# Rotating the next group's queries right behind their product, ahead of the squares and of gating, in a fused gated-attention and feed-forward kernel

## The reference, cut to what matters

```python
# 16 sequences of 64 tokens, 256 wide; 16 query heads in 4 groups, head width 128
xn = layernorm(x)
q = rms_norm(xn @ wq, q_norm_w); k = rms_norm(xn @ wk, k_norm_w); v = xn @ wv
k_ctx = rms_norm(ctx @ wk_ctx, k_norm_w); v_ctx = ctx @ wv_ctx
q = q * cos + rotate_half(q) * sin          # the rotation; k likewise, k_ctx not
scores = q @ concat(k_ctx, k).T / sqrt(128) + causal_mask
x = x + tanh(g_xattn) * (softmax(scores) @ concat(v_ctx, v)).flat @ wo
h = layernorm(x)                            # the weights below rounded to 8-bit floats
x = x + tanh(g_ffn) * ((silu(h @ gate * gs) * (h @ up * us)) @ down * ds)
```

## Time and profile before

| | |
|---|---|
| three runs | 312.31, 312.32, 313.82 us; median 312.32 |
| the profiled execution | 312.29 us, of which the span from first to last instruction is 310.2 us |
| TensorE clock granted | 1.00 of full speed in the whole span |
| busy: PE, DVE, ACT, POOL | 294.8 (95%), 229.4 (74%), 232.2 (75%), 180.8 us (58%) |
| HBM | 40 GB/s over the span; transfers are dense only in its first eighth |

### The profile page before, as it was taken

The page is one execution under the profiler, slowest core; times in us unless marked ns, Lnnn a source line. Parts: engine busy times, 40 slices in busy tenths (PEclk is TensorE's granted clock), DMA queues, the critical chain, the costliest instruction groups (busy, mean ns, idle before and its releaser), DMA issues.

```text
span 310.2 us, 6558 instructions
## 1 busy us (share of the span) xinstructions
PE 294.8 (95%) x2231; PEld 234.8 (76%) x2231; DVE 229.4 (74%) x481; ACT 232.2 (75%) x893; POOL 180.8 (58%) x177
## 2 busy tenths in 40 slices
PE   6896989998999999999999999999999999988876
PEld 3354656675877888888888888888888888877765
DVE  1668998889888898769875787758775976676553
ACT  2468687887789978888977768787887778776632
POOL 1225695567747687457955586457755685556330
PEclk9999999999999999999999999999999999999999
DMA  6999000000000010000000010000000000000001
GB/s 200 389 389 394 15 17 2 0 1 2 18 3 0 1 36 2 0 0 21 19 0 2 0 37 0 2 1 20 0 3 0 2 17 4 2 0 19 0 0 36
DMA packets 6720, 12.84 MB, mean 41 GB/s; under 512 B 800, under 2 KB 4256, under 8 KB 6688
## 3 DMA queue, kind: packets, MB, share of 16 engines
q1 hardware_dynamic: 6688, 12.43, 11.3%
HBM read 11.38 MB, written 1.05 MB: 40 GB/s over the span
## 4 chain that ended last, share of the span: by engine, by line
PE 31%; ACT 27%; DVE 25%; issue 8%; POOL 6%; DMA 2%; SPq 1%; DVEq 0%; POOLq 0%
ACT probs L932 10%; ACT squares L768 6%; PE ps_y L444 5%; DVE row_max L1217 4%; DVE exp_bias L1220 3%; DVE q_sin L1082 3%; PE ps_attn L737 3%; PE ps_transposed L430 3%; ACT qt L852 3%; PE ps_scores L693 3%; DVE q_rot L1078 2%; PE ps_kv L418 2%; ACT const L825 2%; PE ps_probs L430 2%; DMA const<-in_constants_dram 2%
## 5 line engine op out<-in xcount | busy, mean ns | idle before, releaser
L932 ACT ACTIVATE probs<-ps_scores,exp_bias,q_scale 128x128 f32<-128x128 f32 x128 | 57.0, 456 | 26.5 <-DVE exp_bias L1220 26.4
L1395 POOL TENSOR_TENSOR q_rot<-q_rot,q_sin 128x512 f32<-128x512 f32 x31 | 39.7, 1281 | 17.6 <-DVE q_sin L1082 17.5
L1439 POOL TENSOR_TENSOR probs<-probs,row_inv 128x512 f32<-128x512 f32 x32 | 36.3, 1134 | 19.0 <-DVE row_inv L1273 19.0
L1346 POOL TENSOR_TENSOR q_scale<-ssq_eps,minus_half 128x4 f32<-128x4 f32 x32 | 38.8, 1213 | 10.5 <-DVE ssq_eps L1243 9.8
L1357 POOL TENSOR_TENSOR fuse_lo<-fuse,fuse_hi 128x256 fp32r<-128x256 f32 x21 | 15.4, 733 | 41.8 <-ACT fuse_hi L777 41.8
L768 ACT ACTIVATE squares<-ps_q 128x128 bf16<-128x128 f32 x128 | 34.1, 292 | 5.9 <-PE ps_q L412 4.1
L737 PE MATMUL ps_attn<-pt,values 128*128 128x256 f32 x128 | 33.4, 383 | 0.0
L693 PE MATMUL ps_scores<-kt,qt 128*64 128x128 f32 x512 | 33.3, 273 | 0.0
L1078 DVE TENSOR_TENSOR q_rot<-ps_q,rope 128x512 f32<-128x512 f32 x31 | 21.2, 684 | 11.9 <-ACT squares L768 11.9
L693 PEld LDWEIGHTS ps_scores<-kt,qt 128*64 128x64 f32 x512 | 28.9, 137 | 0.0
L908 ACT ACTIVATE pt<-ps_probs 128x512 f32<-128x512 f32 x32 | 19.2, 600 | 11.8 <-PE ps_probs L430 11.6
(11 more groups left out here) (190 smaller groups left out, 832.0 us busy)
## 6 DMA issues: line engine op xcount, KB each, us to landing
q_raw<-in_wq_dram SPq DMA_DIRECT2D x4, 512.0 KB, 8.7
o_raw<-in_wo_dram SPq DMA_DIRECT2D x4, 512.0 KB, 11.6
ctx_t<-in_ctx_dram SPq DMA_DIRECT2D x8, 128.0 KB, 2.6
out_dram<-x_sb SPq DMA_DIRECT2D x8, 128.0 KB, 1.9
stage<-in_gate_w_dram SPq DMA_DIRECT2D x2, 384.0 KB, 10.4
stage<-in_up_w_dram SPq DMA_DIRECT2D x2, 384.0 KB, 11.4
x_sb<-in_x_dram SPq DMA_DIRECT2D x1, 768.0 KB, 13.4
stage<-in_down_w_dram SPq DMA_DIRECT2D x2, 384.0 KB, 13.1
```

The lines of the kernel that those rows point to most:

```text
L932: last = nc.scalar.activation(probs[:, i, :], ps_s[:, i * P:(i + 1) * P], ACT.Exp, bias=exp_bias[:, i:i + 1], scale=q_scale[:, k % 2, i:i ...
L1346: return nc.gpsimd.tensor_tensor(dst, src, minus_half[:, 0:src.shape[1]], ALU.pow)
L1395: nc.gpsimd.tensor_tensor(q_rot[:, :, :], q_rot[:, :, :], q_sin[:, :, :], ALU.add)\
L1439: nc.gpsimd.tensor_tensor(probs[:, :, :], probs[:, :, :], row_inv[:, :].unsqueeze(2).broadcast_to([P, 4, P]), ALU.mult).then_inc(probs_rea ...
```

## The change

It moves three things and turns one dependence round. VectorE rotates the queries of k + 1 as soon as their product is made (`q_made`), ahead of the next tile's norm, `k_var`, gating and the keys' rotation; only `ot_lo` and, at j = 2, L1147 stay in front. ScalarE's squares of the same queries wait for the rotation (`q_sin_ready`) where the rotation waited for them; TensorE's next product into `ps_q` waits for the squares, and `ssq_eps` too. GpSimd adds the queries ahead of `fuse_rest` and the keys' sum. ScalarE makes `x2t_hi` ahead of the keys' squares. No instruction is added or removed.

```diff
--- before.py
+++ after.py
@@ -642,10 +642,7 @@
                     g1 = (k + 1) % GROUPS
                     p1 = ((k + 1) // GROUPS) % 2
                     if is_step(u, k):
-
-                        pe.wait_ge(q_sin_ready, step(u, k) + 1)
-                    if at_step(u, k) == 0:
-                        pe.wait_ge(q_squared, 1)
+                        pe.wait_ge(q_squared, step(u, k) + 1)
                     q_tile = tile(u, (k + 1) // GROUPS)
                     is_native = native("q", g1, q_tile)
                     weights_ready("q", g1, q_tile)
@@ -800,7 +797,7 @@
                 m, j = divmod(k, GROUPS)
                 par, nxt = m % 2, (m + 1) % 2
                 if is_step(u, k + 1):
-                    act.wait_ge(q_made, step(u, k + 1) + 1)
+                    act.wait_ge(q_sin_ready, step(u, k + 1) + 1)
                     if is_step(u, k):
                         act.wait_ge(ssq_moved, step(u, k) + 1)
 
@@ -875,6 +872,11 @@
                 if not after_last:
                     fuse_high(u, FF_LATE.get(k - 1))
 
+                if j == 2 and is_tile(u, m - 1):
+                    act.wait_ge(x2_turned, tile(u, m - 1) + 1)
+                    nc.scalar.activation(x2t[0][:, (m - 1) % 2, :, :].rearrange("p c n -> p (c n)"), ps_t[:, 0:HID], ACT.Copy)\
+                        .then_inc(x2_hi_ready, 1)
+
                 if j == 2 and is_tile(u, m + 1):
                     t1 = tile(u, m + 1)
 
@@ -893,10 +895,6 @@
                     if tile(u, m + 1) >= TOKENS_SPLIT_FROM:
                         nc.scalar.activation(xt[0][:, nxt, 0:KC, :].rearrange("p c n -> p (c n)"), ps_t[:, 0:HID], ACT.Copy)\
                             .then_inc(xt_hi_ready, 1)
-                if j == 2 and is_tile(u, m - 1):
-                    act.wait_ge(x2_turned, tile(u, m - 1) + 1)
-                    nc.scalar.activation(x2t[0][:, (m - 1) % 2, :, :].rearrange("p c n -> p (c n)"), ps_t[:, 0:HID], ACT.Copy)\
-                        .then_inc(x2_hi_ready, 1)
                 if j == 3 and is_tile(u, m + 1):
                     act.wait_ge(ks_turned, tile(u, m + 1) + 1)
                     nc.scalar.activation(kt[:, nxt, :, 0:4:3, :],
@@ -1072,7 +1070,7 @@
                 par, nxt = m % 2, (m + 1) % 2
                 if is_step(u, k + 1):
 
-                    dve.wait_ge(q_squared, step(u, k + 1) + 1)
+                    dve.wait_ge(q_made, step(u, k + 1) + 1)
                     if is_step(u, k):
                         dve.wait_ge(q_turned, step(u, k) + 1)
                     nc.vector.tensor_tensor(q_rot[:, :, :], four(ps_q), over_heads(rope[:, 0, :]), ALU.mult)\
@@ -1148,6 +1146,8 @@
                                             ALU.subtract, ALU.mult).then_inc(x2_ready, 1)
 
 
+                rotate_queries(u, k)
+
                 if j == 3 and is_tile(u, m + 2):
                     dve.wait_ge(ln_inv_ready, tile(u, m + 2) + 1)
 
@@ -1186,8 +1186,6 @@
                         dve.wait_ge(ks_turned, tile(u, m) + 1)
                     nc.vector.tensor_tensor(kn[:, :, :], four(kv_bank(u, m + 1, 0)),
                                             k_inv[:, :].unsqueeze(2).broadcast_to([P, HPG, DIM]), ALU.mult).then_inc(kc_ready, 1)
-
-                rotate_queries(u, k)
 
                 if j == 2 and is_tile(u, m - 1):
                     dve.wait_ge(x2_hi_ready, tile(u, m - 1) + 1)
@@ -1240,6 +1238,7 @@
                 if is_step(u, k + 1):
                     if is_step(u, k):
                         dve.wait_ge(q_scale_ready, step(u, k) + 1)
+                    dve.wait_ge(q_squared, step(u, k + 1) + 1)
                     nc.vector.tensor_scalar(ssq_eps[:, :], ssq[:, :], DIM * RMS_EPS, None, ALU.add)\
                         .then_inc(ssq_moved, 1)
 
@@ -1380,6 +1379,12 @@
                     inverse_root(k_inv[:, :], k_var[:, :]).then_inc(kc_inv_ready, 1)
 
 
+                if is_step(u, k + 1):
+                    pool.wait_ge(q_sin_ready, step(u, k + 1) + 1)
+                    nc.gpsimd.tensor_tensor(q_rot[:, :, :], q_rot[:, :, :], q_sin[:, :, :], ALU.add)\
+                        .then_inc(q_rot_ready, 1)
+
+
                 fuse_rest(u, FF_LATE.get(k - 1))
 
 
@@ -1388,12 +1393,6 @@
                     pool.wait_ge(ks_roped, t1 + 1)
                     nc.gpsimd.tensor_tensor(k_cos[:, :, :], k_cos[:, :, :], k_sin[:, :, :], ALU.add)\
                         .then_inc(ks_added, 1)
-
-
-                if is_step(u, k + 1):
-                    pool.wait_ge(q_sin_ready, step(u, k + 1) + 1)
-                    nc.gpsimd.tensor_tensor(q_rot[:, :, :], q_rot[:, :, :], q_sin[:, :, :], ALU.add)\
-                        .then_inc(q_rot_ready, 1)
 
 
                 if ROUND_AT.get(k - 1, 0) >= WIDE:
```

## The result

The changed kernel takes 320.55 us (median of 4 runs, 319.69 to 320.57) against 312.31 us before: ratio 1.0246, 95% interval 1.0225 to 1.0267. The forecast was 318.7 us in a range of 315.5 to 321.5; the measured loss is 8.2 us where 6.4 were summed. The profiled execution took 320.57 us, of which the span is 318.4 us; before it was 312.29 and 310.2.

What follows compares the result with a forecast made beforehand. The prediction took TensorE, busy without a gap in steps 10 to 27, as the bound; 5.3 + 0.9 + 0.6 - 0.4 = +6.4 us on 312.3 gave 318.7 us, range 315.5 to 321.5.

Steps and rivals of the forecast that it cites:

- TensorE sets the pace of the middle: Steps 10 to 27: TensorE is busy throughout, so nothing ahead of it gains time; only a new wait loses some.
- The rival that the loop sets the pace: Steps 10 to 27: the chain's loop, not TensorE, sets step time; 10.4 us less, about 302 us; chance 5%.
- Steps with j = 2: Steps 10, 14, 18, 22, 26: TensorE waits for late keys' squares; +5.3 us, bounds 4.0 and 6.5.
- The prediction's estimate by the Trainium skill: Five j = 2 steps: if each VectorE operation waits for an empty pipe, 1.5 us more; not adopted.
- Steps with j = 1: Steps 17, 21, 25: `k_var` behind the rotation delays the context keys 0.3 us each; +0.9, bounds 0 and 1.5.
- Gating, `exp_bias`, GpSimd: nothing in the middle: Middle steps: gating's delay stays within 1.46 us of cover; earlier `exp_bias` and later GpSimd work change nothing.
- The first steps: 17 to 104 us: `q_rot` wait goes, step 1 gives it back, later squares delay TensorE; +0.6, bounds -2.0 and +3.
- the prediction's own sign: First 104 us: the forecast counts as wrong if this stretch changes by more than 2 us.
- The last steps: After the middle: waits for `qt` and L1147 shrink, most lost again in the last rotation step; -0.4, bounds -1.5 and +0.5.

Runs made afterwards that it cites:

- e8: Changed kernel with the new order and dependence only in steps with j = 2, the old one in all others: 318.50 us.
- e1: Changed kernel with the old order and dependence in steps with j = 2 alone: 313.41 us, ratio to before 1.0024.
- e7: Kernel before, with VectorE at j = 2 multiplying the keys by cosines and sines once more into spare buffers, ahead of the keys' rotation: 319.82 us.
- e2: Changed kernel with the old order and dependence in steps with j = 1 alone: 316.63 us.
- e6: Changed kernel with GpSimd's sum and `x2t_hi` back at their old places in every step: 321.48 us.
- e3: Changed kernel with the old order and dependence in step 1 alone: 318.17 us.
- e4: Changed kernel with six added TensorE multiplications of ones in step 1, ahead of its wait for the context keys: 318.82 us.
- e5: Changed kernel with the new order and dependence only in steps with j = 0 and j = 3, the old one otherwise: 309.72 us, ratio to before 0.9918.

## Why the prediction was right, point by point

**TensorE sets the pace of the middle.** Shown. Steps 15, 19, 23 and 27 take 8.56 us in all kernels shown, whatever ScalarE, VectorE and GpSimd do, and ScalarE's shorter wait for `exp_bias` bought nothing there. The exponentials did start 0.8 to 1.1 us sooner behind their scores in the steps from 15 to 27 with j = 3, 0 and 1 (0.3 later with j = 2). The rival that the loop sets the pace had to make such steps shorter by 0.8 us; steps 16, 20 and 24 got 0.05 shorter, as they did in e8, where their order is the old one.

The Trainium skill's caution against the matmul busy share ("Perfetto Trace Analysis", section "Identifying the Most-Contended Engine") did not bear here: a weight-load share of 87% came with no room for orders on the other engines.

**Steps with j = 2: +5.3.** Step 18's chain was forecast nearly start for start: rotation 0.09 us behind the product's end (0.04 measured, since L1145 was early), TensorE 4.81 us behind the query product measured and 4.81 forecast. That the two agree to the last digit is luck: the rotation came 0.05 us early and the handover to TensorE, 0.1 by choice, took 0.14. The five steps lengthened by 0.77 and 4 x 1.13, 5.3 in all. Shown by e1 (undone alone), e8 (done alone) and e7 (the pair alone).

The prediction's estimate by the Trainium skill, 1.5 us more over the five steps, did not come: the scaling starts 1.20 us behind the rotation, as in the rows before. The same section, "The DRAIN you can't avoid" in "VectorE: DVE Perf Modes", adds that a next operation that is not held starts earlier, which the prediction left out; so the rows don't speak against the page.

**Steps with j = 1: +0.9.** 0.08 in step 13 and 3 x 0.32, 1.05 in all; shown by e2.

**Gating, `exp_bias`, GpSimd: nothing in the middle.** Right, by the rows of step 20, the waits, and e6.

**The first steps: +0.6.** This is the term that was mis-sized: from step 0 to 10 it measured +2.2. By the prediction's own sign, a change of more than 2 us in the first 104, this part of the forecast was wrong, although the total was not. The waits came nearly as taken, which is in part luck, since +0.6 was an estimate with no row for each step behind it: -0.7 for `q_rot`, +0.8 in step 1, -0.9 for GpSimd's late division in step 3, +0.9 for the context keys in step 5 and +0.4 in steps 2 and 6, together about +0.5. What the sum lacked is the clock. I gave back in step 1 what was won in step 0, and looked at when the keys come, not at how long TensorE stands idle before them: 1.33 us before, 2.52 after, and behind that the granted clock fell to half for 3.4 us, at 1.7 us (e3, e4). The +2.2 stayed in the bounds that I gave, -2 to +3, which had no term for the clock.

**The last steps: -0.4.** -0.6. What `exp_bias` gives is mostly lost again, by two waits. The one that was forecast is in step 31: TensorE's wait for `qt` grew from 0.74 to 1.24 us behind the step with the rotation at j = 2 (it is 0.74 in e5, which has the old order there). The other, 0.69 us for `fuse_lo` in step 29, was not forecast, so the size is right in part by luck.

**The remainder** is the 0.5 us by which step 0 began later in the profiled execution, which no term had. The long first product that makes it is in four of the ten profiles, whatever the order.

## What to carry to other kernels

Where one engine is busy without a gap, moving work forward on another can hardly gain and can lose; ask which signal of the full engine has the least slack (here 0.16 us, the keys' squares) and what the moved work now stands in front of. An order that is harmful in two of four kinds of steps can be worth keeping in the other two: measured apart, j = 0 and 3 gave 0.8% and j = 1 and 2 took it and more. Count a new idle stretch of TensorE at the start twice, once for itself and once for what the clock may do behind it; the second is a chance and not a certainty.

## What the runs showed of the hardware that was not expected

Behind 2.52 us without work TensorE was granted 1.2 GHz for 3.4 us, in all four runs of the changed kernel (granted clock 0.995; only the profiled run shows where) but only in five of eight of e1 and three of four of e6, which have the same idle stretch. The four 128x512 products then took 3.19 us instead of 1.88. Behind 1.33 us (e2, e3, e5, e8) and behind 1.55 us with six small matrix products ahead of them (e4) it kept 2.4 GHz in all 21 runs. The idle stretch is not the only way to such a drop, though. One of four runs of e7 and, of the 19 runs of the kernel before made beside the experiments at a clock above 0.99, two had a granted clock of 0.994 or 0.995, with 1.33 us idle in their profiles; the two took 313.62 and 313.81 us. Where the clock fell in them no profile shows.

VectorE's `exp_bias`, 128x4 elements, ran 0.59 us in step 0 of the changed kernel and 0.16 in step 1; where it was long it ended with GpSimd's sum (23.22 and 23.21 us). Before it took over 0.3 us in 26 of 32 steps and ended within 0.03 us of GpSimd's sum in 25 of them. With the earlier sum it did so in 13, and in 11 of these it ended with another operation of GpSimd (`fuse_lo`, or the rounding of weights at L1366). So an earlier sum frees it only where nothing else of GpSimd's stands there. The multiplies of the rotations, which read PSUM, kept to 0.65 to 0.69 us in all ten profiles, overlapped by GpSimd or not. In all, the same 481 VectorE instructions were busy for 229.4 us before and 216.8 after.
